# Order of the twelve matmuls of a piece, and the place of the wait for the low half

## What is computed

```
h   = maximum(layernorm(x, axis=-1), 0)
out = x + (1 - 0.1) * (adj @ h) + 0.1 * L0_gnn_h
```

## Time and profile before

| | |
|---|---|
| median of 3 runs | 733.97 us (733.93 to 733.99) |
| span of the profiled execution, first to last instruction | 732.3 us |
| median less span, what lies around it | 1.7 us |
| TensorE matmul busy | 719.5 us, 98% |
| TensorE weight load busy | 571.9 us, 78% |
| VectorE busy | 601.7 us, 82% |
| ScalarE busy | 504.6 us, 69% |
| DMA | 281.19 MB, 384 GB/s over the span |
| granted TensorE clock, mean | 0.999 of full speed |

### The profile page before, as it was taken

One profiled execution on the slowest core, in us unless ns is written; L12 is line 12 of the kernel. 1 busy time (PEld: TensorE's weight loads), 2 busy tenths in 40 slices (PEclk: granted clock), 3 DMA queues, 4 the chain that ended last, 5 costly groups with the idle time before them and its releaser, 6 DMA issues.

```text
span 732.3 us, 9026 instructions
## 1 busy us (share of the span) xinstructions
PE 719.5 (98%) x3072; PEld 571.9 (78%) x3072; DVE 601.7 (82%) x456; ACT 504.6 (69%) x335; POOL 0.7 (0%) x6
## 2 busy tenths in 40 slices
PE   5999999999999999999999999999999999999998
PEld 2444888888888888888888888888888888888886
DVE  6843988888888888888888888888888888888885
ACT  5763767677676676777677676676777677676773
POOL 0000000000000000000000000000000000000000
PEclk9999999999999999999999999999999999999999
DMA  9998999999899999979999997999999899999990
GB/s 366 420 421 322 402 422 401 398 377 412 319 414 422 419 410 380 414 299 405 424 420 413 381 404 306 402 422 422 421 379 398 306 398 424 422 421 384 392 383 14
DMA packets 42493, 281.19 MB, mean 384 GB/s; under 512 B 4720, under 2 KB 4720, under 8 KB 9456
## 3 DMA queue, kind: packets, MB, share of 16 engines
q1 hardware_dynamic: 42480, 281.04, 95.1%
HBM read 276.82 MB, written 4.19 MB: 384 GB/s over the span
## 4 chain that ended last, share of the span: by engine, by line
PE 98%; DVE 1%; DMA 0%; ACT 0%; issue 0%; DVEq 0%
PE acc L339 30%; PE acc L335 30%; PE acc L336 30%; PE acc L318 8%; PE x_t L308 1%; DMA x_sb<-x_dram 0%; DVE a_lo L292 0%; ACT h_full L191 0%; DVE stats L241 0%; DVE finished L274 0%; DVE mean_var L244 0%; ACT std L188 0%; DVE rstd L249 0%; DVE var_eps L247 0%; DVE newton L252 0%
## 5 line engine op out<-in xcount | busy, mean ns | idle before, releaser
L292 DVE TENSOR_TENSOR a_lo<-raw,a_hi 128x2048 fp32r<-128x2048 f32 x240 | 549.6, 2292 | 92.1 <-ACT a_hi L216 92.1
L216 ACT ACTIVATE a_hi<-raw 128x2048 fp32r<-128x2048 f32 x240 | 461.0, 1921 | 204.1 <-PE acc L339 191.0
L335 PE MATMUL acc<-a_hi,h_hi 128*128 128x512 f32 x960 | 375.1, 391 | 0.0
L336 PE MATMUL acc<-a_hi,h_lo 128*128 128x512 f32 x960 | 373.7, 389 | 0.0
L339 PE MATMUL acc<-a_lo,h_hi 128*128 128x512 f32 x960 | 256.9, 389 | 1.3 <-DVE a_lo L292 1.3
L339 PEld LDWEIGHTS acc<-a_lo,h_hi 128*128 128x128 f32 x960 | 180.1, 188 | 39.2 <-DVE a_lo L292 1.7
L336 PEld LDWEIGHTS acc<-a_hi,h_lo 128*128 128x128 f32 x960 | 180.3, 188 | 37.0
L335 PEld LDWEIGHTS acc<-a_hi,h_hi 128*128 128x128 f32 x960 | 180.2, 188 | 37.0
L318 PE MATMUL acc<-raw,h_full 128*128 128x512 f32 x128 | 58.7, 620 | 8.3 <-ACT h_full L191 8.3
L318 PEld LDWEIGHTS acc<-raw,h_full 128*128 128x128 f32 x128 | 25.2, 199 | 41.0 <-issue 31.9
L191 ACT ACTIVATE h_full<-x_sb,shift,rstd 128x128 f32<-128x128 f32 x64 | 25.4, 480 | 9.0 <-DVE shift L254 9.0
(11 more groups left out here) (14 smaller groups left out, 9.9 us busy)
## 6 DMA issues: line engine op xcount, KB each, us to landing
raw<-adj_dram SPq DMA_DIRECT2D x256, 1024.0 KB, 6.2
h_sb<-h_dram SPq DMA_DIRECT2D x16, 256.0 KB, 6.2
out_dram<-finished SPq DMA_DIRECT2D x16, 256.0 KB, 6.5
x_sb<-x_dram SPq DMA_DIRECT2D x2, 1024.0 KB, 15.5
x_sb<-x_dram SPq DMA_DIRECT2D x3, 512.0 KB, 8.8
x_sb<-x_dram SPq DMA_DIRECT2D x2, 256.0 KB, 4.0
```

The lines of the kernel that those rows point to most:

```text
L216: nc.scalar.activation(a_hi[:, local % SPLIT_SLOTS, :], raw[:, raw_slot(local), :], ACT.Copy).then_inc(hi_ready, 1)
L292: low = nc.vector.tensor_tensor(a_lo[:, local % SPLIT_SLOTS, :], raw[:, raw_slot(local), :], a_hi[:, local % SPLIT_SLOTS, :].bitcast(fp32) ...
L335: nc.tensor.matmul(bank, h_hi[:, k, :], hi[:, cols], start=(k == 0), stop=False)
L336: nc.tensor.matmul(bank, h_lo[:, k, :], hi[:, cols], start=False, stop=False)
```

## The change

Inside a piece, TensorE's twelve matmuls are put in another order. Before, they were `h_hi`·`a_hi` and `h_lo`·`a_hi` for each of the four blocks, then the wait for `lo_ready`, then `h_hi`·`a_lo` for the four blocks. After, each block's three matmuls stand together, as `h_lo`·`a_hi`, `h_hi`·`a_hi`, `h_hi`·`a_lo`, so that the two with stationary operand `h_hi` are neighbours. The wait for `lo_ready` is behind the second matmul of the first block, ahead of the third matmul of the piece. The number of matmuls, their operands, the semaphores and the programs of the other engines are as they were.

```diff
                         pe.wait_ge(hi_ready, split_through(i, local))
-                        for k, cols in blocks:
-                            nc.tensor.matmul(bank, h_hi[:, k, :], hi[:, cols], start=(k == 0), stop=False)
-                            nc.tensor.matmul(bank, h_lo[:, k, :], hi[:, cols], start=False, stop=False)
-                        pe.wait_ge(lo_ready, split_through(i, local))
-                        for k, cols in blocks:
+                        for n, (k, cols) in enumerate(blocks):
+                            nc.tensor.matmul(bank, h_lo[:, k, :], hi[:, cols], start=(k == 0), stop=False)
+                            nc.tensor.matmul(bank, h_hi[:, k, :], hi[:, cols], start=False, stop=False)
+                            if n == 0:
+                                pe.wait_ge(lo_ready, split_through(i, local))
                             last = nc.tensor.matmul(bank, h_hi[:, k, :], lo[:, cols],
                                                     start=False, stop=(k == BLOCKS - 1))
                         last.then_inc(piece_used, 1)
```

## The result

The changed kernel took 736.95 us in the median of six runs (735.35 to 737.05), the kernel before 733.98 (733.93 to 734.18) beside it. The ratio is 1.0033 with a 95% interval of 1.0022 to 1.0045, so by the prediction's own line of 0.2% it is slower, and just clear of it. The forecast was 735.35 in a range of 734.6 to 737.0, with "same" as the likeliest verdict. The range held the median by 0.05 us; the likeliest case was not the commonest one.

A forecast was written before the change was run, and what follows sets the result against it. TensorE's matmul count and spacing were taken to bound the kernel. Steady part and repeated loads 0, one longer stall in piece 16 1.4 us: span 732.3 + 1.4 = 733.7, with 1.7 us around it 735.35 us, range 734.6 to 737.0.

The forecast's parts named there:

- the prediction's own line of 0.2%: Whole kernel: about 0.2%, 1.47 us, is what a measurement can tell from no change.
- the likeliest case: Piece 16: a single longer stall and nothing else, 735.35 us, own range 735.1 to 735.7, chance 0.70.
- The place and size of the stall: Piece 16: TensorE stands until 70.56, six matmuls pushed behind the wait, 1.36 to 1.39 us lost.
- No further stall: Pieces 17 to 19: low half ready before it is wanted, slack growing from 0.7 us, so one stall only.
- The steady part at nothing: The other 239 pieces: the earlier wait finds its semaphore raised, 1.36 us in hand, cost 0.
- The repeated load at nothing: All pieces: two loads in a row bring in the same `h_hi`, none falls away, gain taken as nothing.
- the rival's 724.1 us: Split pieces: the 960 repeated loads are saved, 11.2 us faster, chance 0.11.
- The prediction's other estimate, 10.5 us: Split pieces: saving if 960 repeated loads went away, 10.9 ns each by the skill's 216 ns.
- The clock: Stall near 68 us: rival in which the clock falls to half, 1.5 us more, 736.9 us, chance 0.13.
- The other sentence: Stall in piece 16: its 2.66 us exceed the 2.1 us after which the clock fell at the run's end.
- The rival's price: Clock falling in the stall: 1.5 us, the middle between nothing and 3 us for six us at half clock.
- the lower half of this rival: Clock falling in the stall: its times up to 737.0 us, which carry the forecast's range to 0.78.

The follow-up runs named there:

- Experiment 1: The kernel before, its matmul order kept, with only the wait for the low half moved ahead of the third matmul: 735.54 us, ratio 1.0029.
- first_piece_old: The changed kernel with the old order and old wait place in the first piece of each loop turn alone (5 of 240): 735.00 us against 734.02.
- experiment 2: The changed kernel with old order and wait place in the first chunk of each loop turn (734.09 us), or in its first piece alone (735.00 us).
- Experiment 5: Chunk 0's transposes moved after piece 12: changed kernel 732.55 us, kernel before 732.51 us, old order with the wait ahead of the first matmul 732.46 us.
- experiment 4: The kernel before with only the low-half wait moved: ahead of the fifth matmul 736.49 us, ahead of the first 735.83 to 738.74 us.

## Why the prediction was right, and where it was wrong

**The place and size of the stall: right.** One stall, in piece 16, TensorE back at 70.55 (70.56 before), six matmuls behind it. Experiment 1 puts piece 17 at 72.97 for the forecast's 73.0, and 1.36 us on the time for 1.36 to 1.39.

**No further stall: right.** Piece 17 had 0.45 us from its start to its third matmul and the low half was there. `first_piece_old` in experiment 2 shows how near it was: there piece 17 starts at 71.85 instead of 72.97, in a profile in which all that comes before is 0.25 us later, so about 1.4 us earlier against VectorE, and it stalls.

**The steady part at nothing: right.** Experiment 5 is the test, since it takes away the only late `a_lo` and leaves 240 waits in their new places: no difference, even ahead of the first matmul.

**The repeated load at nothing: right.** 3072 loads are left, the spacing is 0.227 us, and the rival's 724.1 us is 13 us away. The prediction's other estimate, 10.5 us, goes by the 216 ns that the Trainium skill (TensorE: Matmul & The Clock Gate, Back-to-back issue gap) gives for a matmul by itself; the loads were not dropped, so no run here shows whether that spacing could be had. The same section also gives about 131 ns for 512 columns in a stream with loads; the traces, at 226.7 ns, do not bear that out for this kernel's fp32r matmuls.

**The clock: the step that failed.** The rival was there, with a chance of 0.13, and it was the commonest run. The chance was too low because of the sentence set against it, that at the end of the run no work followed the idle time "while here the matmuls come back". In the changed kernel's profile the clock falls at about 70.48, just ahead of TensorE's return at 70.55, and in the two profiles of experiment 4 it falls 0.6 and 1.0 us after the return. The other sentence, that the new stall of 2.66 us is longer than the 2.1 us after which the clock fell at the end of the run, pointed the right way, but it was one case, and the 2.1 us are no fixed delay. At the end of the changed kernel's own profile the last matmul ends at 732.01, and the clock is still at full when the span ends, 3.2 us later:

```profile
734.00:735.20 1.20, 0.00 (x0) 0.00 (x0) 0.00 (x0) 0.00 (x0) 0.00 (x0) 1.00 0.27 101
```

What the runs show in place of 0.13 is 17 falls in the 29 runs with a stall of 2.2 to 3.2 us (6 of 11, 3 of 7, 4 of 6, 4 of 5). No row of the kernel before could have given that number.

**Where luck helped.** The rival's price, 1.5 us against 1.56 measured, was the middle between nothing and 3 us, and the 3 us stood for 6 us at half clock in chunk 0; here the low level lasted from 70.5 to 73.9. And the median lies in whichever group is the larger. With four runs of six in the clock's group it came to 736.95, inside the range only because the range went up to 737.0 for the lower half of this rival. The single number, 735.35, was that of the smaller group (735.35 and 735.50 measured).

**What stays open.** The same 2.7 us of idle time end in a fall in one run and not in the next. The moment at which the level changes differs from run to run in chunk 0 too, as the last section shows; whether this decides about the stall was not tested.

## What to carry to other kernels

A wait that never waits in the steady part still has a price at its first turn, where the pipeline fills: count the instructions that it pushes behind that one late arrival. A stall of the engine that sets the time is worth removing at its root, here one place in an order written by hand, before any order behind it is tuned. When an order makes a stall on TensorE longer, ask for the clock as well (here 1.3 us of stall never had a fall in 77 runs, and 2.2 us had one in 6 of 11), and read single runs and not only the median.

## What had not been expected of the hardware

Idle time of TensorE can cost more than its own length, and only sometimes: 2.7 us of stall against 1.3 added 1.4 us in some runs and 2.9 to 3.1 in others. Nor does the program fix the moment at which the clock rises. In chunk 0 of the profiled run of before the full level came between 13.61 and 14.88 us; in the changed kernel, whose chunk 0 is the same, it came near 12.5, as the weight loads show:

```profile
12.21 0.32 PEld L318 LDWEIGHTS acc<-raw,h_full 128*128 128x128 f32 x1 [0.52 <-issue]
12.77 0.19 PEld L318 LDWEIGHTS acc<-raw,h_full 128*128 128x128 f32 x1 [0.24 <-issue]
```

Both moments are read from the spacing of the loads, 0.86 or 0.43 us. The column PEclk can't be used there: it says 1.00 in the profile of before even while the spacing is 0.86:

```profile
13.00:14.00 1.00, 1.00 (x2) 0.42 (x2) 0.90 (x5) 0.30 (x1) 0.00 (x0) 1.00 1.01 426
```

The earlier rise puts TensorE 0.83 us ahead (the twelfth load starts at 14.91 us and had started at 15.74), yet the transposes behind chunk 0 start at 66.83 us and had started at 66.84. The waits of the changed kernel have one on a transfer that the matmuls of before do not have:

```profile
PE acc L318 <- DMA raw<-adj_dram: 0.8, 1, 0.8
```

The changed kernel's page, part 4, says the same in the chain that ended last, by line:

```profile
PE acc L339 30%; PE acc L335 30%; PE acc L336 30%; PE acc L318 6%; DMA raw<-adj_dram 3%; PE x_t L308 1%; SPq L156 0%; DVE a_lo L292 0%; SPq L150 0%; DVE finished L274 0%; DVEq L285 0%; DVE residual L267 0%; DVEq L291 0%; DVEq L266 0%
```

It has 3% of the span on the transfers of `raw`, where the earlier trace rows have none, and 6% on line 318 for 8%. So, as far as the profiles tell, chunk 0 gives such a gain away to the transfers: of the eight with the transposes at the end of chunk 0, seven start them between 66.81 and 66.88 us, and the eighth, of the run at 735.34 us, at 67.09. That this is why the time of before hardly varies is likely, but only one of its runs has a profile.
